# The scan of the state space layer: VectorE scales the last token tile of u times B, ScalarE the other seven

## The chip, the core and the metric

One core of a Trainium2 chip runs the whole program. The metric is the time of one execution on the device in microseconds (us). One execution was profiled; all rows of this document before the prediction come from it.

## The reference, cut to what matters

Four layers are chained, each with a residual: attention, a ternary feed-forward layer, a state space layer (Mamba) and a 2:4 sparse feed-forward layer. The change is in the third. Its input is (2, 1024, 256), there are 512 channels d and 16 states n:

```python
delta = softplus(dt_low @ dt_proj.T + bias)          # (b, l, 512)
deltaA = exp(delta[..., d] * A[d, n])                # decay per state
dBu = delta[b, l, d] * Bm[b, l, n] * x_conv[b, l, d] # drive per state
h = deltaA * h + dBu                                 # over the tokens l
y = sum over n of h * C[b, l, n]                     # then skip, gate, projection
```

With u = delta * x_conv, the drive of state n is u times B[:, n], one factor per token.

## The kernel before, in words

The two batches are worked off one after the other. Channels lie on the 128 partitions, in four tiles of 128; 1024 tokens lie along a row. A batch is scanned in two halves of two channel tiles each (e = 0, 1). A half has 16 states, in four rings (`it`) of four (`v`). One state of a half is a *pair* of two *units* (e = 0 and e = 1), so a batch has 32 pairs and 64 units, numbered by `unit`. For each unit:

- ScalarE, `decays` (L1424): the exponentials of 128x1024 into one of four buffers `m_da`. Semaphore `da_done`.
- ScalarE, `spread` (L1418): the factor B is one per token, so u is kept transposed (`m_uT`, tokens on the partitions, eight token tiles of 128x256 for both channel tiles) and each tile is scaled by one scalar per partition into `m_uB`, eight operations per pair. `m_uB` has two buffers; `spread` waits for `db_done`, the expands that read the buffer last. Semaphore `ub_done`, one count per tile.
- TensorE, `expand` (L907 to L914): eight transposes (128x128) bring the scaled tiles back to channels on partitions, into PSUM banks 4 to 7 (`drive(e)`). It waits for the scan that last read these banks, and with e = 0 before each transpose for its tile of `m_uB`. Semaphore `db_done`.
- VectorE, `state` (L2146 to L2156): a scan along the 1024 tokens, state = decay times state plus drive, into one of four buffers `m_h`. It waits for `da_done`, `db_done` and an add four units back. Semaphore `scan_done`.
- GpSimd (L2406): the product of the state with the row of C in place (`m_C`, one load by SyncE's queue per pair, L422). Semaphore `hc_done`.
- TensorE, `add_state` (L919): four matmuls with the identity add the product to y in PSUM. Semaphore `y_added`.

All engines work in the order in which their loops are written. On TensorE it is expand of a unit, then add of the unit two back. On VectorE it is scan after scan, and in half 1 the operations that finish the channels of half 0 stand between them: skip 0 and skip 1 (L2186, behind the first and the second scan of the half), gate 0 (L2192, before iteration 1), gate 1 (in iteration 1), low part 0 (L2196, before iteration 2), low part 1 (in iteration 2), and in batch 1 the statistics of the next layer before iteration 3. Gates and low parts read two tensors in SBUF, the skips one in SBUF and one in PSUM. ScalarE runs decays of pair v, then the spread of pair v + 1.

Elsewhere, VectorE and GpSimd meet in the attention layer: VectorE computes a bias row (L1531, a tensor times one scalar per partition) while GpSimd clips scores (L2279).

Of the kernel before, what the change touches and what calls it, by code (L numbers as in the profile page):

```python
# [12 lines left out]
ALU = mybir.AluOpType  # L13
# [4 lines left out]
B, S, D = 2, 1024, 256  # L18
KD = D // P
TILES = S // P  # L20
# [6 lines left out]
DI, DN, DR, DC = 512, 16, 128, 4  # L27
DT = DI // P
RING = 4
QUAD = 4  # L30
UNITS = 2 * B * TILES // QUAD
HALF_UNITS = DN * 2
# [8 lines left out]
def program(nc, x_in, slopes_in, wqk_in, wv_in, wo_in, wgu0_in, wp0_in, win_in, wx_in, wdt_in,  # L41
# [3 lines left out]
    with ctx:  # L45
# [82 lines left out]
        def causal_row(k):  # L128
# [72 lines left out]
        m_uT = place(t_mem, "m_uT", [P, 2, TILES, 2 * P])  # L201
# [63 lines left out]

        (mw_in, mw_hi, mw_lo, m_pad, m_in_full, m_in_read, m_z_read, m_tap, m_conv, m_silu, m_xc_hi, m_xc_lo, m_xd_full,
         m_xd_read, m_xd_lo, m_bc_out, m_dt_full, m_dt_act, m_sp, m_pre, bt_full, bt_read, ut_full, ut0_read, ut1_read,
         c_in0, c_in1, c_in2, c_in3, da_done, ub_done,
         db_done, scan_done, hc_done, y_added, y_skip, yz_done, y_hi, y_lo, m_o_full, m_o_added) = (
            sem(n) for n in (  # L270
                "mw_in", "mw_hi", "mw_lo", "m_pad", "m_in_full", "m_in_read", "m_z_read", "m_tap", "m_conv", "m_silu",
                "m_xc_hi", "m_xc_lo", "m_xd_full", "m_xd_read", "m_xd_lo", "m_bc_out", "m_dt_full", "m_dt_act",
                "m_softplus", "m_pre", "bt_full", "bt_read", "ut_full", "ut0_read", "ut1_read",
                "c_in0", "c_in1", "c_in2", "c_in3", "da_done", "ub_done", "db_done",
                "scan_done", "hc_done", "y_added", "y_skip", "yz_done", "y_hi", "y_lo", "m_o_full", "m_o_added"))
        c_in = (c_in0, c_in1, c_in2, c_in3)

# [16 lines left out]
        def unit(b, half, it, v, e):  # L294

            return it * (2 * RING) + ((2 * b + half) * HALF_UNITS + 2 * v + e)

        def drive(e):
            return ps[:, 4 + 2 * e:6 + 2 * e, :].rearrange("p a n -> p (a n)")
# [603 lines left out]
        def pe_mamba_scan(pe, b):  # L903

            def expand(half, it, v, e):

                n = unit(b, half, it, v, e)  # L907
                pe.wait_ge(scan_done, n + 3)
                for t in range(TILES):
                    if e == 0:  # L910
                        pe.wait_ge(ub_done, n * (TILES // 2) + (t + 1))
                    mm = nc.tensor.transpose(ps[:, 4 + 2 * e + t // 4, (t % 4) * P:(t % 4 + 1) * P],  # L912
                                             m_uB[:, v % 2, t, e * P:(e + 1) * P], ident[:, :])
                mm.then_inc(db_done, 1)  # L914

            def add_state(half, it, v, e, begin=False, end=False):
                pe.wait_ge(hc_done, unit(b, half, it, v, e) + 1)
                for c in range(2):
                    mm = nc.tensor.matmul(ps[:, 2 * e + c, :], ident[:, :],  # L919
                                          m_h[:, 2 * (v % 2) + e, c * BANK:(c + 1) * BANK],  # L920
                                          start=begin, stop=end)
                mm.then_inc(y_added, 1)

            last = DN // RING - 1
            for half in range(2):
                for e in range(2):
                    expand(half, 0, 0, e)
                    if half:
                        add_state(0, last, RING - 1, e, end=True)
                for v in range(1, RING):  # L930
                    for e in range(2):
                        expand(half, 0, v, e)
                        if half and v == 1:
                            pe.wait_ge(y_skip, DT * b + e + 1)
                        add_state(half, 0, v - 1, e, begin=(v == 1))
                with pe.Fori(1, last + 1) as it:
                    for v in range(RING):
                        for e in range(2):
                            expand(half, it, v, e)
                            if v:  # L940
                                add_state(half, it, v - 1, e)
                            else:
                                add_state(half, it - 1, RING - 1, e)
            for e in range(2):
                add_state(1, last, RING - 1, e, end=True)
                if b == B - 1:
                    pe.wait_ge(scan_done, 4 + 2 * B * HALF_UNITS)
                    pe_mamba_out(pe, b, (0, 1), range(4 * e, 4 * e + 4))
# [463 lines left out]
        def act_mamba_scan(act, b):  # L1412
            last = DN // RING - 1

            def spread(half, it, v):
                act.wait_ge(db_done, unit(b, half, it, v, 0) + 2)
                for t in range(TILES):
                    nc.scalar.activation(m_uB[:, v % 2, t, :], m_uT[:, half, t, :], ACT.Copy,  # L1418
                                         scale=m_bT[:, t, bass.ds(it * RING + v, 1)]).then_inc(ub_done, 1)

# [726 lines left out]
        def dve_mamba_scan(dve, b):  # L2147

            def state(half, it, v, es=range(2)):
                for e in es:  # L2150
                    n = unit(b, half, it, v, e)
                    dve.wait_ge(da_done, n + 1)
                    dve.wait_ge(y_added, n + 5)
                    dve.wait_ge(db_done, n + 5)
                    nc.vector.tensor_tensor_scan(m_h[:, 2 * (v % 2) + e, :], m_da[:, 2 * (v % 2) + e, :], drive(e),  # L2155
                                                 0.0, ALU.mult, ALU.add).then_inc(scan_done, 1)  # L2156

            with dve.Fori(0, DN // RING) as it:
                for v in range(RING):
                    state(0, it, v)  # L2160
            for e in range(2):
                state(1, 0, 0, (e,))
                dve.wait_ge(y_added, 8 + (2 * b + 1) * HALF_UNITS - 1 + e)
                dve_mamba_skip(dve, b, e)
            for v in range(1, RING):
                state(1, 0, v)
            dve_mamba_gate(dve, b, 0)
            for v in range(RING):
                state(1, 1, v)
                if v == 1:  # L2170
                    dve_mamba_gate(dve, b, 1)
                if v == 3:
                    dve_mamba_y_lo(dve, b, 0)
            for v in range(RING):
                state(1, 2, v)
                if v == 1:
                    dve_mamba_y_lo(dve, b, 1)
                if v == 3 and b == B - 1:
                    dve_sparse_stats(dve, 0)
            with dve.Fori(3, DN // RING) as it:  # L2180
                for v in range(RING):
                    state(1, it, v)

        def dve_mamba_skip(dve, b, e):
            at = 2 * (e % 2)
            nc.vector.scalar_tensor_tensor(m_xc[:, e, :], m_xc[:, e, :], skip_d[:, e:e + 1],  # L2186
                                           ps[:, at:at + 2, :].rearrange("p a n -> p (a n)"),
                                           ALU.mult, ALU.add).then_inc(y_skip, 1)
# [5 lines left out]
        def dve_mamba_y_lo(dve, b, e):  # L2194
            dve.wait_ge(y_hi, DT * b + e + 1)
            nc.vector.tensor_tensor(m_yl[:, e, :], m_xc[:, e, :], m_yh[:, e, :].bitcast(F32),  # L2196
                                    ALU.subtract).then_inc(y_lo, 1)
# [294 lines left out]
```

## Time and profile before

| | before |
|---|---|
| median of 3 runs | 1737.82 us (1734.57 to 1737.91) |
| the profiled execution | 1736.06 us, its span 1734.2 us |
| TensorE matmul / weight load | 1651.6 us (95%) / 1368.0 us (79%) |
| VectorE, ScalarE, GpSimd | 1395.4 (80%), 1266.7 (73%), 761.7 us (44%) |
| scan operation, VectorE | 128 times, mean 2.283 us, 291.0 us |
| product with C, GpSimd | 128 times, mean 2.422 us, 309.3 us |
| scaling of a token tile, ScalarE | 512 times, 210.6 us |
| chain that ended last | PE 62%, POOL 18%, DVE 10%, issue 6% of the span |

PE is TensorE, PEld its weight loads, DVE VectorE, ACT ScalarE, POOL GpSimd, SP SyncE. A row of the timeline has the start in us, the duration in us, the engine, the line, the operation with output and inputs, the count, and in brackets the idle time just before it with what released it. Where several instructions follow closely, one row holds them all.

### The profile page before, as it was taken

Reading aid. Unit: us, or ns where it says so; the run is one execution under the profiler, and the core shown is the slowest. Engines: PE = TensorE matmul, PEld = TensorE weight load, DVE = VectorE, ACT = ScalarE, POOL = GpSimd, SP = SyncE. Lnnn points to the kernel's source line nnn. Section 1 sums busy time; section 2 is a strip of 40 time slices with the busy share of each in tenths; the row PEclk is TensorE's granted clock in tenths of the full one; section 3 lists DMA queues with packets and bytes.
Section 4 is the critical chain, followed back from the end, with each engine's and each line's share of the span. In section 5 each row is a group of like instructions: output and inputs, shape, how many; then the busy total and the mean of one; then the engine's idle time right before and its main releaser. Section 6 shows DMA issues by size and latency. Waiting matters only on the chain.

```text
span 1734.2 us, 31419 instructions
## 1 busy us (share of the span) xinstructions
PE 1651.6 (95%) x9564; PEld 1368.0 (79%) x9564; DVE 1395.4 (80%) x2319; ACT 1266.7 (73%) x2380; POOL 761.7 (44%) x717
## 2 busy tenths in 40 slices
PE   8999999999999999999997997879999899999998
PEld 7899889998899889988995886656557656557887
DVE  7788877887787778777886665888988788888996
ACT  5777777777777777777774553899996799994442
POOL 4444435453544444444442111049893079881000
PEclk9999999999999999999999998989999999999999
DMA  2000000000000000000001000022220032240000
GB/s 99 31 20 19 30 24 18 18 30 24 16 16 28 24 21 11 25 24 27 9 0 50 1 0 0 4 85 98 97 97 13 13 112 97 98 138 8 13 13 25
DMA packets 25105, 64.13 MB, mean 37 GB/s; under 512 B 2832, under 2 KB 8976, under 8 KB 24784
## 3 DMA queue, kind: packets, MB, share of 16 engines
q1 hardware_dynamic: 25040, 63.31, 10.8%
q8 instruction: 36, 0.59, 0.1%
q14 instruction: 29, 0.24, 0.0%
HBM read 60.94 MB, written 2.36 MB: 36 GB/s over the span
## 4 chain that ended last, share of the span: by engine, by line
PE 62%; POOL 18%; DVE 10%; issue 6%; ACT 2%; DMA 1%; POOLq 0%; DVEq 0%; SPq 0%; ACTq 0%
POOL m_h L2406 15%; PE ps L565 11%; PE ps L527 10%; PE ps L550 7%; PE ps L482 7%; PE ps L578 5%; PE ps L505 5%; PE ps L781 4%; PE ps L697 3%; PE ps L793 2%; PE ps L718 2%; POOL prob L2286 1%; PE ps L957 1%; DVE m_delta L2096 1%; POOL prob L2279 1%
## 5 line engine op out<-in xcount | busy, mean ns | idle before, releaser
L2406 POOL TENSOR_TENSOR m_h<-m_h,m_C 128x1024 f32<-128x1024 f32 x128 | 309.3, 2422 | 174.2 <-DVE m_h L2155 173.6
L2155 DVE TENSOR_TENSOR_SCAN m_h<-m_y,ps 128x1024 f32<-128x1024 f32 x128 | 291.0, 2283 | 44.8 <-PE ps L912 42.8
L2286 POOL TENSOR_SCALAR prob<-prob,rinv 128x128 f32<-128x128 f32 (+7 forms) x256 | 228.4, 899 | 212.9 <-DVE rinv L1611 206.5
L2279 POOL TENSOR_SCALAR prob<-prob 128x128 f32<-128x128 f32 (+7 forms) x256 | 188.2, 735 | 286.2 <-ACT prob L1048 277.7
L919 PE MATMUL ps<-m_h,ident 128*128 128x512 f32 x512 | 246.0, 603 | 11.2 <-POOL m_h L2406 11.1
L1577 DVE TENSOR_TENSOR pt_lo<-ps,pt_hi 128x512 fp32r<-128x512 f32 (+2 forms) x320 | 189.6, 605 | 80.9 <-ACT pt_hi L1061 79.1
L1570 DVE CUSTOM_DVE_ANT_0 prob<-prob,bias 128x128 f32<-128x128 f32 (+7 forms) x256 | 214.0, 854 | 7.8 <-POOL prob L2279 4.6
L1048 ACT ACTIVATE prob<-ps 128x128 f32<-128x128 f32 (+7 forms) x256 | 165.7, 652 | 67.3 <-PE ps L527 66.7
L1061 ACT ACTIVATE pt_hi<-ps 128x512 fp32r<-128x512 f32 (+2 forms) x320 | 163.0, 531 | 66.4 <-PE ps L550 64.4
L1418 ACT ACTIVATE m_u<-m_uT,m_bT 128x256 f32<-128x256 f32 x512 | 210.6, 495 | 0.3 <-PE ps L912 0.2
L1054 ACT ACTIVATE prob<-prob,nmax 128x128 f32<-128x128 f32 (+7 forms) x256 | 198.1, 776 | 3.0 <-DVE nmax L1570 2.0
L912 PEld LDWEIGHTS ps<-ident,m_u 128*128 128x128 f32 x1024 | 122.7, 143 | 74.1 <-issue 60.6
L550 PE MATMUL ps<-ident,prob 128*128 128x128 f32 x1152 | 159.4, 274 | 7.1 <-POOL prob L2286 4.0
L550 PEld LDWEIGHTS ps<-ident,prob 128*128 128x128 f32 x1152 | 135.1, 141 | 29.2 <-issue 7.2
L919 PEld LDWEIGHTS ps<-m_h,ident 128*128 128x128 f32 x512 | 88.1, 192 | 79.7 <-issue 63.8
L527 PE MATMUL ps<-qk_hi 128*128 128x512 f32 (+2 forms) x384 | 143.4, 373 | 4.5 <-DVE v_lo L1583 2.4
L912 PE MATMUL ps<-ident,m_u 128*128 128x128 f32 x1024 | 136.5, 277 | 7.2 <-DVE m_uT L2143 5.0
L1424 ACT ACTIVATE m_y<-m_delta,negA 128x1024 f32<-128x1024 f32 x128 | 139.3, 1136 | 0.0
L527 PE MATMUL ps<-qk_hi,qk_lo 128*128 128x512 f32 (+2 forms) x384 | 131.9, 343 | 0.0
L527 PE MATMUL ps<-qk_lo,qk_hi 128*128 128x512 f32 (+2 forms) x384 | 131.4, 342 | 0.0
L565 PE MATMUL ps<-pt_hi,v_hi 128*128 128x512 f32 (+2 forms) x320 | 116.5, 364 | 0.0
L565 PE MATMUL ps<-pt_lo,v_hi 128*128 128x512 f32 (+2 forms) x320 | 115.7, 362 | 0.0
(257 smaller groups left out, 3961.7 us busy)
## 6 DMA issues: line engine op xcount, KB each, us to landing
m_C<-bc_dram SPq DMA_DIRECT2D x64, 512.0 KB, 3.6
wqk_raw<-wqk_in SPq DMA_DIRECT2D x16, 512.0 KB, 3.2
wv_raw<-wv_in SPq DMA_DIRECT2D x16, 256.0 KB, 2.6
wo_raw<-wo_in SPq DMA_DIRECT2D x16, 256.0 KB, 2.8
q_raw<-wgu_in SPq DMA_DIRECT2D x8, 256.0 KB, 2.7
raw<-wgu_in SPq DMA_DIRECT2D x1, 2048.0 KB, 8.0
out<-x SPq DMA_DIRECT2D x8, 256.0 KB, 2.1
x<-x_in SPq DMA_DIRECT2D x2, 512.0 KB, 4.3
```

Source lines behind the costliest of these rows:

```text
L527: mm = nc.tensor.matmul(flat[:, o + lo_c:o + hi_c], (qk_hi, qk_lo)[a][:, 2 * u, qt * P:(qt + 1) * P], (qk_hi, qk_lo)[w][:, 2 * u + 1, lo_c ...
L550: mm = nc.tensor.transpose(ps[:, 4 + idx % 2, r * P:(r + 1) * P], prob[:, at:at + P], ident[:, :])
L565: mm = nc.tensor.matmul(ps[:, 6 + g, c0:BANK], (v_hi, v_lo)[w][:, j, u * DH:(u + 1) * DH], cols, start=(j == 0 and i == 0), stop=(j == 4 * ...
L912: mm = nc.tensor.transpose(ps[:, 4 + 2 * e + t // 4, (t % 4) * P:(t % 4 + 1) * P], m_uB[:, v % 2, t, e * P:(e + 1) * P], ident[:, :])
L919: mm = nc.tensor.matmul(ps[:, 2 * e + c, :], ident[:, :], m_h[:, 2 * (v % 2) + e, c * BANK:(c + 1) * BANK], start=begin, stop=end)
L1054: nc.scalar.activation(prob[:, at:at + n], prob[:, at:at + n], ACT.Exp, bias=nmax[:, k:k + 1], scale=-1.0, accum_out=rsum[:, k:k + 1]).the ...
L1418: nc.scalar.activation(m_uB[:, v % 2, t, :], m_uT[:, half, t, :], ACT.Copy, scale=m_bT[:, t, bass.ds(it * RING + v, 1)]).then_inc(ub_done, 1)
L1570: nc.vector.tensor_tensor_reduce(out=tile, in0=tile, in1=bias[:, k // 8, S - n:S], scale=-1.0, scalar=BIG, op0=ALU.add, op1=ALU.min, accum ...
L2155: nc.vector.tensor_tensor_scan(m_h[:, 2 * (v % 2) + e, :], m_da[:, 2 * (v % 2) + e, :], drive(e), 0.0, ALU.mult, ALU.add).then_inc(scan_do ...
L2279: nc.gpsimd.tensor_scalar(prob[:, at:at + n], prob[:, at:at + n], CLIP, -CLIP, ALU.min, ALU.max).then_inc(s_clipped, 1)
L2286: nc.gpsimd.tensor_scalar(prob[:, at:at + n], prob[:, at:at + n], rinv[:, k:k + 1], 1.0, ALU.mult, ALU.mult).then_inc(norm_done, 1)
L2406: nc.gpsimd.tensor_tensor(state, state, m_C[:, v, :], ALU.mult).then_inc(hc_done, 1)
```

## The change

VectorE scales the eighth token tile, with a semaphore of its own, `ub_last`; ScalarE's loop ends at the seventh. On VectorE the scaling of pair v + 1 stands between the two scans of pair v (`both`) for v = 0 to 2. For v = 3 the scaling of the first pair of the next ring stands behind both scans. The loops over the rings are cut so that the last ring of a half is written out or ends without a scaling behind it. TensorE waits for `ub_done` before seven transposes and for `ub_last` before the eighth.

```diff
--- before.py
+++ after.py
@@ -265,13 +265,13 @@
 
         (mw_in, mw_hi, mw_lo, m_pad, m_in_full, m_in_read, m_z_read, m_tap, m_conv, m_silu, m_xc_hi, m_xc_lo, m_xd_full,
          m_xd_read, m_xd_lo, m_bc_out, m_dt_full, m_dt_act, m_sp, m_pre, bt_full, bt_read, ut_full, ut0_read, ut1_read,
-         c_in0, c_in1, c_in2, c_in3, da_done, ub_done,
+         c_in0, c_in1, c_in2, c_in3, da_done, ub_done, ub_last,
          db_done, scan_done, hc_done, y_added, y_skip, yz_done, y_hi, y_lo, m_o_full, m_o_added) = (
             sem(n) for n in (
                 "mw_in", "mw_hi", "mw_lo", "m_pad", "m_in_full", "m_in_read", "m_z_read", "m_tap", "m_conv", "m_silu",
                 "m_xc_hi", "m_xc_lo", "m_xd_full", "m_xd_read", "m_xd_lo", "m_bc_out", "m_dt_full", "m_dt_act",
                 "m_softplus", "m_pre", "bt_full", "bt_read", "ut_full", "ut0_read", "ut1_read",
-                "c_in0", "c_in1", "c_in2", "c_in3", "da_done", "ub_done", "db_done",
+                "c_in0", "c_in1", "c_in2", "c_in3", "da_done", "ub_done", "ub_last", "db_done",
                 "scan_done", "hc_done", "y_added", "y_skip", "yz_done", "y_hi", "y_lo", "m_o_full", "m_o_added"))
         c_in = (c_in0, c_in1, c_in2, c_in3)
 
@@ -294,6 +294,10 @@
         def unit(b, half, it, v, e):
 
             return it * (2 * RING) + ((2 * b + half) * HALF_UNITS + 2 * v + e)
+
+        def pair(b, half, it, v):
+
+            return it * RING + ((2 * b + half) * (HALF_UNITS // 2) + v)
 
         def drive(e):
             return ps[:, 4 + 2 * e:6 + 2 * e, :].rearrange("p a n -> p (a n)")
@@ -907,8 +911,10 @@
                 n = unit(b, half, it, v, e)
                 pe.wait_ge(scan_done, n + 3)
                 for t in range(TILES):
-                    if e == 0:
-                        pe.wait_ge(ub_done, n * (TILES // 2) + (t + 1))
+                    if e == 0 and t < TILES - 1:
+                        pe.wait_ge(ub_done, pair(b, half, it, v) * (TILES - 1) + (t + 1))
+                    elif e == 0:
+                        pe.wait_ge(ub_last, pair(b, half, it, v) + 1)
                     mm = nc.tensor.transpose(ps[:, 4 + 2 * e + t // 4, (t % 4) * P:(t % 4 + 1) * P],
                                              m_uB[:, v % 2, t, e * P:(e + 1) * P], ident[:, :])
                 mm.then_inc(db_done, 1)
@@ -1414,7 +1420,7 @@
 
             def spread(half, it, v):
                 act.wait_ge(db_done, unit(b, half, it, v, 0) + 2)
-                for t in range(TILES):
+                for t in range(TILES - 1):
                     nc.scalar.activation(m_uB[:, v % 2, t, :], m_uT[:, half, t, :], ACT.Copy,
                                          scale=m_bT[:, t, bass.ds(it * RING + v, 1)]).then_inc(ub_done, 1)
 
@@ -2155,31 +2161,61 @@
                     nc.vector.tensor_tensor_scan(m_h[:, 2 * (v % 2) + e, :], m_da[:, 2 * (v % 2) + e, :], drive(e),
                                                  0.0, ALU.mult, ALU.add).then_inc(scan_done, 1)
 
-            with dve.Fori(0, DN // RING) as it:
+            def spread_last(half, it, v):
+
+                dve.wait_ge(db_done, unit(b, half, it, v, 0) + 2)
+                dve.sem_inc(seen, 1)
+                nc.vector.tensor_scalar(m_uB[:, v % 2, TILES - 1, :], m_uT[:, half, TILES - 1, :],
+                                        m_bT[:, TILES - 1, bass.ds(it * RING + v, 1)], None,
+                                        ALU.mult).then_inc(ub_last, 1)
+
+            def both(half, it, v):
+
+                state(half, it, v, (0,))
+                if v < RING - 1:
+                    spread_last(half, it, v + 1)
+                state(half, it, v, (1,))
+
+            last = DN // RING - 1
+            dve.wait_ge(ut0_read, 2 * (b + 1))
+            dve.wait_ge(bt_read, b + 1)
+            spread_last(0, 0, 0)
+            with dve.Fori(0, last) as it:
                 for v in range(RING):
-                    state(0, it, v)
+                    both(0, it, v)
+                spread_last(0, it + 1, 0)
+            for v in range(RING):
+                both(0, last, v)
+            dve.wait_ge(ut1_read, 2 * (b + 1))
+            spread_last(1, 0, 0)
             for e in range(2):
                 state(1, 0, 0, (e,))
                 dve.wait_ge(y_added, 8 + (2 * b + 1) * HALF_UNITS - 1 + e)
                 dve_mamba_skip(dve, b, e)
+                if e == 0:
+                    spread_last(1, 0, 1)
             for v in range(1, RING):
-                state(1, 0, v)
+                both(1, 0, v)
+            spread_last(1, 1, 0)
             dve_mamba_gate(dve, b, 0)
             for v in range(RING):
-                state(1, 1, v)
+                both(1, 1, v)
                 if v == 1:
                     dve_mamba_gate(dve, b, 1)
                 if v == 3:
+                    spread_last(1, 2, 0)
                     dve_mamba_y_lo(dve, b, 0)
             for v in range(RING):
-                state(1, 2, v)
+                both(1, 2, v)
                 if v == 1:
                     dve_mamba_y_lo(dve, b, 1)
-                if v == 3 and b == B - 1:
-                    dve_sparse_stats(dve, 0)
-            with dve.Fori(3, DN // RING) as it:
+                if v == 3:
+                    spread_last(1, 3, 0)
+                    if b == B - 1:
+                        dve_sparse_stats(dve, 0)
+            with dve.Fori(last, DN // RING) as it:
                 for v in range(RING):
-                    state(1, it, v)
+                    both(1, it, v)
 
         def dve_mamba_skip(dve, b, e):
             at = 2 * (e % 2)
```

## Rows read from the trace of the kernel before

**Rows 1.** Windows: busy time (and count) of each engine in a steady stretch.

```profile
core 0: us, PE busy (x) PEld busy (x) DVE busy (x) ACT busy (x) POOL busy (x), PEclk, DMA share, GB/s
1156.00:1228.00 72.00, 72.00 (x333) 43.91 (x332) 63.44 (x29) 72.00 (x139) 65.57 (x28) 1.00 0.29 102
```

**Rows 2.** Timeline of all engines, steady stretch of half 0, batch 0.

```profile
1158.71 2.17 ACT L1424 ACTIVATE m_y<-m_delta,negA 128x1024 f32<-128x1024 f32 x2
...
1158.93 1.88 PE L919 MATMUL ps<-m_h,ident 128*128 128x512 f32 x4
1158.97 2.37 POOL L2406 TENSOR_TENSOR m_h<-m_h,m_C 128x1024 f32<-128x1024 f32 x1 [0.23 <-DVE m_h L2155]
1159.20 2.29 DVE L2155 TENSOR_TENSOR_SCAN m_h<-m_y,ps 128x1024 f32<-128x1024 f32 x1 [0.31 <-PE ps L912]
...
1160.65 1.04 PE L912 MATMUL ps<-ident,m_u 128*128 128x128 f32 x8
...
1160.79 3.29 ACT L1418 ACTIVATE m_u<-m_uT,m_bT 128x256 f32<-128x256 f32 x8
...
1161.52 1.88 PE L919 MATMUL ps<-m_h,ident 128*128 128x512 f32 x4
...
1161.79 2.29 DVE L2155 TENSOR_TENSOR_SCAN m_h<-m_y,ps 128x1024 f32<-128x1024 f32 x1 [0.31 <-PE ps L912]
...
1163.98 2.18 ACT L1424 ACTIVATE m_y<-m_delta,negA 128x1024 f32<-128x1024 f32 x2
```

**Rows 3.** Timeline around gate 0, batch 0.

```profile
1248.93 2.29 DVE L2155 TENSOR_TENSOR_SCAN m_h<-m_y,ps 128x1024 f32<-128x1024 f32 x1 [0.31 <-PE ps L912]
...
1251.13 1.20 DVE L2192 TENSOR_TENSOR m_xc<-m_xc,m_z 128x1024 f32<-128x1024 f32 x1
...
1251.29 7.99 POOL L2406 TENSOR_TENSOR m_h<-m_h,m_C 128x1024 f32<-128x1024 f32 x3 [0.23 <-DVE m_h L2155]
...
1252.25 4.46 DVE L2155 TENSOR_TENSOR_SCAN m_h<-m_y,ps 128x1024 f32<-128x1024 f32 x2
...
1254.61 1.98 PE L919 MATMUL ps<-m_h,ident 128*128 128x512 f32 x4 [0.63 <-POOL m_h L2406]
...
1257.30 1.88 PE L919 MATMUL ps<-m_h,ident 128*128 128x512 f32 x4
...
1260.19 2.29 DVE L2155 TENSOR_TENSOR_SCAN m_h<-m_y,ps 128x1024 f32<-128x1024 f32 x1 [0.30 <-PE ps L912]
```

**Rows 4.** Single lines: min/median/max ns; last row: a group (busy us, mean ns).

```profile
L1531 DVE TENSOR_SCALAR bias<-ramp,slopes x30: 737/744/1620, 58.4 to 892.7; 128x1024 f32<-128x1024 f32 x30
...
L1515 DVE TENSOR_SCALAR a_xn<-x,mv,rstd x8: 401/406/817, 28.6 to 31.3; 128x256 f32<-128x256 f32 x8
...
L2139 DVE TENSOR_TENSOR m_delta<-m_delta,m_l 128x1024 f32<-128x1024 f32 x8 | 9.8, 1225 | 0.3
```

**Rows 5.** Timeline in the attention layer, VectorE's bias row and GpSimd's clip.

```profile
892.70 1.62 DVE L1531 TENSOR_SCALAR bias<-ramp,slopes 128x1024 f32<-128x1024 f32 x1
892.73 1.04 POOL L2279 TENSOR_SCALAR prob<-prob 128x1024 f32<-128x1024 f32 x1
```

**Rows 6.** Timeline around skip 0, batch 0.

```profile
1231.43 1.26 DVE L2186 SCALAR_TENSOR_TENSOR m_xc<-m_xc,vecs,ps 128x1024 f32<-128x1024 f32 x1
...
1231.59 2.37 POOL L2406 TENSOR_TENSOR m_h<-m_h,m_C 128x1024 f32<-128x1024 f32 x1 [0.25 <-DVE m_h L2155]
...
1232.60 2.28 DVE L2155 TENSOR_TENSOR_SCAN m_h<-m_y,ps 128x1024 f32<-128x1024 f32 x1
...
1237.48 1.96 PE L919 MATMUL ps<-m_h,ident 128*128 128x512 f32 x4 [0.54 <-POOL m_h L2406]
```

**Rows 7.** Windows at the start of the scan of batch 0, columns as in rows 1.

```profile
1145.80:1149.20 3.40, 1.84 (x11) 1.01 (x9) 3.39 (x2) 3.40 (x8) 2.11 (x1) 1.00 0.18 75
1149.20:1152.60 3.40, 3.09 (x4) 1.41 (x5) 2.29 (x1) 3.40 (x8) 3.32 (x3) 0.51 0.00 0
```

**Rows 8.** What VectorE's scans (L2155) waited for: us, times.

```profile
  ACT m_y L1424: 2.0, 6
```

## The prediction

> **What bounds the kernel now.** I read the shares of the page first: TensorE is the busiest engine. The change touches only the scan of the two batches (slices 27 to 36 of 40), so everything else is read there. The windows say who has no air in it: in a stretch of 72.00 us TensorE and ScalarE are both busy 72.00 us, VectorE 63.44, GpSimd 65.57 [rows 1]. The timeline of a steady stretch says which of the two sets the pace [rows 2]. A unit is half a state pair: the expand (eight transposes) starts at 1160.65, the add (four matmuls) at 1161.52, and one add follows the other by 2.59 us (1158.93, 1161.52), as do the scans (1159.20, 1161.79). ScalarE repeats every 5.27 us for two units (1158.71 to 1163.98), 2.635 per unit. A different period, so the units are not paced by ScalarE: it runs ahead and loses 0.09 us a pair of its lead. That TensorE's 2.59 is its own rate and not a latency shows after a gate: adds at 1254.61, 1257.30 and no wait before the second [rows 3]. VectorE idles 0.30 us before each scan; GpSimd's product ends at 1158.97 + 2.37 = 1161.34, 0.18 before its add. So a unit has 0.30 us of air on VectorE, about 0.1 on GpSimd and none on TensorE.
>
> **What is removed.** The two batches have 64 pairs (128 units), and each pair loses one of ScalarE's eight scalings: 3.29/8 = 0.41 us [rows 2], 26 us in all. Nobody waits for them: ScalarE is ahead, and its period drops to 4.87, under TensorE's 5.19. Worth 0.
>
> **What is added, in the common place.** For states 0 to 2 of a ring of four, VectorE's scaling (128x256, one scalar per partition) stands between the two scans of the pair in front. Its price: the bias operation has the same form with 1024 elements and takes 0.744, while a tensor by tensor operation of that size takes 1.225, so it moves two elements in the time of one [rows 4]. Its 1024 elements take 0.55 (what it still had to do when it had been held up, see the gates below), so 768 fewer cost 0.41 less: 0.33, rounded up to 0.34. Above stands the normalisation of the same tile with two scalars, 0.406; below, the part of the bias row that doesn't grow with its length, 0.744 - 0.55 = 0.19. I take 0.34, from the row of the same form. An operation that is ready starts 2.20 us after the scan's start (1248.93 to 1251.13) and the next 0.08 before its end (1251.13 + 1.20 to 1252.25) [rows 3]. So the scaling runs from 2.20 to 2.54, and the second scan could start at 2.46, before its turn at 2.59. Hidden by VectorE's idle time. Its wait (the expands that read the buffer two pairs back) was met two units earlier; nothing is queued behind it but the second scan. The counting and address instructions that come with it are not in these rows; they can run while the first scan streams for 2.29 us, so 0, and up to 0.13 would still be covered. TensorE counts two semaphores where it counted one: 0, hidden by its own matmuls. No DMA is moved; the rows of C wait for adds and shift with them.
>
> On GpSimd the product of the first scan would start at 2.36, inside the scaling. How that is paid is seen at the gate: the product issued at 1251.29 while the gate ran (to 1252.33), and the add behind it started at 1254.61, 2.28 after the gate's end [rows 3]. Here that gives 2.54 + 2.28 = 4.82; the add's turn is at 2.37 + (1161.52 - 1158.97) = 4.92. Hidden, with 0.1 to spare. The Trainium skill (SBUF — State Buffer, section Who interferes with whom) has a harder rule: a VectorE operation on both ports locks GpSimd out for the whole instruction. By it the add would start at 2.54 + 2.37 + 0.05 = 4.96, 0.04 late, at most 0.04 x 32 = 1.3 us more; the gate's row shows an overlap of about 0.15 instead.
>
> **At the end of a ring.** For the first state of the next ring the scaling is written behind the *second* scan, and its reader is the expand that runs during that very scan. That expand starts 1160.65 - 1159.20 = 1.45 into the scan, its eighth transpose at 1.45 + 0.77 = 2.22 (1.04 less one transpose of 0.27 leaves seven steps of 0.11). The tile is done at 2.54, plus a signal of 0.07 (scan end 1251.22 to GpSimd 1251.29), plus a restart of 0 to 0.10 (adds that waited take 1.98, others 1.88 [rows 2, 3]): 0.39 to 0.49 late, I take 0.43. TensorE is in order: the add behind is late too, and with no air nothing gives it back. With the price between 0.19 and 0.406 the stall is 0.24 to 0.56. Places per batch: three rings of half 0, the change of halves, and the rings of half 1 before iterations 1, 2, 3: seven. Two of these have a VectorE operation behind them that reads two tensors (gate 0, low part 0); these are the next part. The very first scaling of a batch runs while TensorE is at its first seven transposes: 0, and 0.34 at most. Five remain: 5 x 0.43 = 2.15 per batch (in batch 1 the statistics stand behind the last, with one input; VectorE's 0.26 more there, the same order).
>
> **Gate 0 and low part 0.** Today the gate starts before GpSimd's product (1251.13, 1251.29) and wins the port. Behind the scaling it can be issued only at 2.46, and the product has stood there since 2.36. Who comes second waits: a bias operation was issued at 892.70, a clip of GpSimd's at 892.73; VectorE's took 1.62 instead of 0.744 and ended 0.55 after GpSimd's end (893.77) [rows 4, 5]. Being issued 0.03 ahead didn't help it, so 0.10 behind will not. Counted from the start of the scan in front: product over at 2.54 + 2.28 less 0.05 for the signal, so about 4.76; gate does its 1024 elements at one each, 0.55 x 2 = 1.08, and ends at 5.84; the next scan starts at 5.76 (now 3.32) and ends at 8.05; the scaling behind it ends at 8.31, its product lets the add go at 8.31 + 2.28 = 10.59, where it now starts at 1257.30 - 1248.93 = 8.37. With the restart the scan two further on is 2.3 late (now 1260.19). The stall of 0.43 lies inside. Two per batch: 4.6.
>
> **Between the skips.** The scaling for state 1 stands behind skip 0, ready at 1232.60, in the middle of the product that runs from 1231.59 to 1233.96 [rows 6]. It waits for that end and needs 0.55/4 = 0.14 more: 1234.10, so the second scan starts at 1234.02 and not 1232.60: 1.42. VectorE is the chain here (the add at 1237.48 waited 0.54 for the product of that scan), so it is passed on: 1.45 with the restart.
>
> **Sum.** 2.15 + 4.6 + 1.45 = 8.2 per batch, 16.4 for both. The profiled execution took 1736.06 (span 1734.2 and 1.9 around it): 1752.5. The three runs have a median of 1737.82, 1.76 more, which gives 1754.2. I forecast **1754**. What follows the scans is released by their last results and moves along.
>
> **Rivals.**
> (a) The clock. After a stretch with TensorE busy 1.84 of 3.40 us at granted 1.00, the next was granted 0.51 (1.2 GHz), and held four matmuls, work of 1.88 us at 2.4 GHz [rows 2, 7]. At the gate and low part TensorE would now stand idle some 2.6 of 3.5 us. Each fall costs up to 1.7: with one to four, 1756 to 1761. Against: idle spells of 0.63 left it at full speed. 0.2.
> (b) The port is no obstacle to gate and skip (the gate keeps it from the scaling, or the scaling takes none). Then a batch loses 5 x 0.43 at ring ends, 0.26 between the skips (the scaling's own time) and at the two gates some 0.15 each, since the late tile falls into TensorE's present wait of 0.63: 2.7, and 5.4 in all. That is 1741.5 from the profiled execution and 1743 from the median. For: gates of before were never locked out for long. Against: rows 5. 0.15.
> (c) GpSimd wins the port in every pair: the scaling then waits for a product of 2.37, some 1.9 us lost in 64 pairs, 120 us, 1858. Its point: the product issued less than some 0.1 after the scaling; it is 0.16. 0.04.
> (d) Not slower: ScalarE is the true bound and TensorE's expand its follower, so that a late eighth tile costs nothing and 0.41 a pair comes off its work. It decides if the eighth scaling ends later than the transposes reach it. For: its 72.00 busy of 72.00 [rows 1]. Against: the two periods differ, and all scans together waited 2.0 us for its decays [rows 8]. That is also about the most to be had: 1735 to 1738. 0.06.
> The rest, 0.05, are mixtures beyond the range. My forecast: 0.5.
>
> **Range.** 1742 (rival b with the cheap scaling) to 1762 (rival a in full); c, d and some mixtures are out, about 0.15. A measurement of this kernel tells about 0.2%, 3.5 us, from no change. Faster 0.02, same 0.05 (d), slower 0.93.
>
> **What would show it.** Steady scans still 2.59 apart inside a ring, and about 3.02 at every ring's end, with TensorE waiting for VectorE's scaling; ScalarE with idle time; scalings of 0.34; gate 0 and low part 0 some 3.4 us long by the row (issued, then waiting) and the scan behind 2.4 later; the scaling between the skips 1.5 long; TensorE's granted clock at 1.00 through both events. Wrong it would be if scans at ring ends stay 2.59 apart, or if gates still take 1.20.

## The result and the profile after

The changed kernel takes **1757.08 us** (median of 4 runs, 1755.75 to 1758.18), the kernel before beside it 1736.81 (4 runs, 1734.57 to 1737.91): a ratio of 1.0123, 95% interval 1.011 to 1.0135, 20 us slower. The forecast was 1754, with 1742 to 1762 as its range. The profiled execution took 1756.45, its span is 1754.7 us.

The head of the page after, with its first part:

```profile
span 1754.7 us, 31475 instructions
## 1 busy us (share of the span) xinstructions
PE 1660.4 (95%) x9564; PEld 1369.7 (78%) x9564; DVE 1422.6 (81%) x2383; ACT 1249.2 (71%) x2316; POOL 761.2 (43%) x717
```

VectorE has 64 instructions more (2319 before), ScalarE 64 fewer: the change does what it says. These shares tell nothing of the 20 us. The steady stretch of [rows 1], as windows of the kernel after, does:

```profile
1156.00:1228.00 72.00, 71.37 (x331) 43.51 (x330) 65.33 (x41) 67.98 (x122) 64.33 (x28) 1.00 0.29 102
```

TensorE, busy 72.00 of 72.00 before, now misses 0.63; ScalarE misses 4.02. The timeline (start, duration, what it waited for) shows where TensorE's 0.63 lies: first two places inside a ring, then the ring's end.

```profile
1156.72 2.29 DVE L2161 TENSOR_TENSOR_SCAN m_h<-m_y,ps 128x1024 f32<-128x1024 f32 x1 [0.31 <-PE ps L918]
...
1158.92 0.33 DVE L2168 TENSOR_SCALAR m_u<-m_uT,m_bT 128x256 f32<-128x256 f32 x1
...
1159.09 2.39 POOL L2442 TENSOR_TENSOR m_h<-m_h,m_C 128x1024 f32<-128x1024 f32 x1 [0.22 <-DVE m_h L2161]
...
1159.31 2.29 DVE L2161 TENSOR_TENSOR_SCAN m_h<-m_y,ps 128x1024 f32<-128x1024 f32 x1
...
1164.50 2.29 DVE L2161 TENSOR_TENSOR_SCAN m_h<-m_y,ps 128x1024 f32<-128x1024 f32 x1 [0.30 <-PE ps L918]
...
1165.95 0.93 PE L918 MATMUL ps<-ident,m_u 128*128 128x128 f32 x7
1166.70 0.33 DVE L2168 TENSOR_SCALAR m_u<-m_uT,m_bT 128x256 f32<-128x256 f32 x1
...
1167.08 0.33 PE L918 MATMUL ps<-ident,m_u 128*128 128x128 f32 x1 [0.21 <-DVE m_u L2168]
...
1167.52 2.29 DVE L2161 TENSOR_TENSOR_SCAN m_h<-m_y,ps 128x1024 f32<-128x1024 f32 x1 [0.49 <-PE ps L918]
```

Inside a ring, scaling and second scan fit: 1156.72 to 1159.31 is the old 2.59. At the ring's end the scaling is issued at 1166.70, when seven of the eight transposes have been issued; the eighth waits for it, and the next scan comes 1167.52 - 1164.50 = 3.02 after the last. Gate 0 and low part 0 (the group for [rows 3]):

```profile
1254.57 0.45 DVE L2168 TENSOR_SCALAR m_u<-m_uT,m_bT 128x256 f32<-128x256 f32 x1
1254.94 3.39 DVE L2228 TENSOR_TENSOR m_xc<-m_xc,m_z 128x1024 f32<-128x1024 f32 x1
...
1277.31 2.29 DVE L2161 TENSOR_TENSOR_SCAN m_h<-m_y,ps 128x1024 f32<-128x1024 f32 x1 [0.31 <-PE ps L918]
1279.51 0.33 DVE L2168 TENSOR_SCALAR m_u<-m_uT,m_bT 128x256 f32<-128x256 f32 x1
1279.67 2.40 POOL L2442 TENSOR_TENSOR m_h<-m_h,m_C 128x1024 f32<-128x1024 f32 x1 [0.23 <-DVE m_h L2161]
1279.75 3.40 DVE L2232 TENSOR_TENSOR m_yl<-m_xc,m_yh 128x1024 fp32r<-128x1024 f32 x1
1283.07 2.27 DVE L2161 TENSOR_TENSOR_SCAN m_h<-m_y,ps 128x1024 f32<-128x1024 f32 x1
```

The gate takes 3.39 instead of 1.20, the low part 3.40. "Locked out" below means just this: issued second at the port of the prediction, and waiting inside one's own row. The low part ends at 1283.15, that is 1.08 after GpSimd's product (1279.67 + 2.40 = 1282.07): it did its 1024 elements when the product was over. The next scan starts 5.76 after the one in front (1277.31 to 1283.07). And between the skips (for [rows 6]):

```profile
1233.41 1.26 DVE L2222 SCALAR_TENSOR_TENSOR m_xc<-m_xc,vecs,ps 128x1024 f32<-128x1024 f32 x1
1233.58 2.37 POOL L2442 TENSOR_TENSOR m_h<-m_h,m_C 128x1024 f32<-128x1024 f32 x1 [0.66 <-DVE m_h L2161]
1234.59 1.51 DVE L2168 TENSOR_SCALAR m_u<-m_uT,m_bT 128x256 f32<-128x256 f32 x1
1236.02 2.27 DVE L2161 TENSOR_TENSOR_SCAN m_h<-m_y,ps 128x1024 f32<-128x1024 f32 x1
```

The scaling takes 1.51 and ends 0.15 after the product (1235.95). The view of its line says how often TensorE's matmuls waited for it, of 64 times:

```profile
L2168 DVE TENSOR_SCALAR m_u<-m_uT,m_bT x64: 321/328/1514, 1142.5 to 1575.2; 128x256 f32<-128x256 f32 x64
...
who waited for it (us, times):
...
  PE ps L918: 3.3, 14
```

Fourteen times: the seven ring ends of two batches. The last part lies in TensorE's clock, which fell in places where it had not fallen before. Windows behind gate 0 of batch 1 (the fields are those of [rows 1]; the third from the end is the granted clock), and below it at that batch's start:

```profile
1514.70:1518.10 3.40, 1.51 (x9) 1.25 (x10) 3.40 (x4) 3.36 (x6) 2.75 (x2) 1.00 0.48 154
1518.10:1521.50 3.40, 3.40 (x7) 1.47 (x6) 2.14 (x2) 0.73 (x1) 3.40 (x2) 0.51 0.00 0
```

```profile
1402.10:1405.50 3.40, 2.95 (x5) 1.36 (x6) 3.26 (x3) 3.40 (x6) 3.33 (x2) 0.50 0.04 13
1405.50:1408.90 3.40, 3.40 (x11) 2.27 (x10) 0.40 (x2) 3.40 (x7) 2.38 (x1) 0.50 0.00 0
```

In the wake of the gate TensorE was busy 1.51 of 3.40 us, and then worked 3.40 us at 1.2 GHz. At the batch's start the clock was at 1.2 GHz for 6.8 us; the kernel before had one stretch of 3.4 after its first scan there (1395.0), and another around the start of that scan (1388.2 to 1391.6, the scan at 1390.63), which the kernel after does not have.

A third place lies behind the scans, at the first matmuls of the next layer. TensorE stands idle there in both kernels alike; in the kernel after, the clock then falls. After, and below it before:

```profile
1600.10:1603.50 3.40, 1.04 (x7) 0.78 (x7) 3.40 (x4) 0.00 (x0) 0.00 (x0) 1.00 0.00 0
1603.50:1606.90 3.40, 3.40 (x10) 2.62 (x9) 1.70 (x3) 0.00 (x0) 0.00 (x0) 0.50 0.02 5
```

```profile
1581.37:1584.77 3.40, 1.04 (x7) 0.78 (x6) 3.40 (x4) 0.00 (x0) 0.00 (x0) 1.00 0.00 0
1584.77:1588.17 3.40, 3.40 (x17) 2.79 (x16) 2.04 (x4) 0.60 (x1) 0.00 (x0) 1.00 0.02 5
```

**Measuring the steps.** Every scan start is a row of the trace, so each place can be read by itself: the time between two scans of one number, after less before. Gate 0 of batch 0, scans 40 and 48: 1252.37 to 1277.31 is 24.94, before 1248.93 to 1271.45 is 22.52: 2.4 more. The same for all places (us more than in the kernel before, batch 0 / batch 1; "start" is scans 1 to 8, "ring ends" scans 8 to 33, "skips" 33 to 40, "gates" 40 to 48, "low parts" 48 to 56, "last ring" 56 to 64):

| kernel | start | ring ends | skips | gates | low parts | last ring | sum |
|---|---|---|---|---|---|---|---|
| after | 0.18 / 1.39 | 1.87 / 1.88 | 1.45 / 1.44 | 2.41 / 3.80 | 2.29 / 2.28 | 0.51 / 0.29 | 8.73 / 11.09 |
| e10, after again | 0.06 / 1.37 | 1.88 / 1.89 | 1.45 / 1.45 | 2.39 / 3.79 | 2.29 / 2.29 | 0.50 / 0.29 | 8.58 / 11.07 |
| e1 | -0.03 / 1.37 | 0.06 / 0.06 | 1.45 / 1.45 | 0.02 / -0.16 | 0.00 / 0.01 | 0.03 / 0.04 | 1.54 / 2.77 |
| e2 | -0.03 / 0.03 | 1.87 / 1.89 | 1.67 / 1.45 | -0.02 / -0.18 | 0.01 / 0.01 | 0.51 / 0.30 | 4.00 / 3.50 |
| e5 | 0.17 / -0.04 | 0.06 / 0.06 | 0.29 / 0.29 | 0.00 / -0.16 | 0.00 / 0.00 | 0.04 / 0.04 | 0.57 / 0.19 |
| e9 | -0.03 / 0.12 | 1.87 / 1.87 | 0.51 / 0.28 | 0.01 / -0.17 | 0.00 / 0.00 | 0.50 / 0.29 | 2.86 / 2.38 |
| e3b | -0.04 / 1.35 | 0.08 / 0.07 | 1.47 / 2.45 | 2.30 / 2.10 | 3.89 / 3.97 | 0.06 / 0.29 | 7.76 / 10.22 |
| e4 | 1.41 / 0.14 | 0.00 / 0.00 | 0.00 / 0.00 | 0.02 / -0.01 | 0.01 / -0.01 | 0.00 / 0.01 | 1.44 / 0.13 |
| e6 | 0.02 / 0.07 | 0.00 / 0.00 | 0.01 / 0.00 | 7.14 / 6.95 | 6.22 / 6.20 | 0.00 / 0.00 | 13.38 / 13.23 |
| e7 | -0.07 / 1.26 | 0.00 / 0.00 | 0.00 / 0.00 | -1.58 / -1.77 | -1.58 / -1.59 | 0.75 / 0.56 | -2.47 / -1.55 |
| e8 | 0.04 / 1.48 | 0.07 / 0.06 | 0.29 / 0.29 | -1.55 / -1.38 | -1.58 / -1.58 | 0.40 / 0.57 | -2.34 / -0.56 |

The first row holds 19.8 of the 20.4 us by which the span grew. The rest lies outside the scans. From the last scan of batch 0 to the first of batch 1 it is 0.96 less, where the kernel before has the extra low stretch, so of the 1.39 at batch 1's start only 0.4 is left. Behind the last scan it is 1.64 more, and that is the third fall of the clock. The same part reads 1.62 in e10, 1.58 in e3b and 1.46 in e9, each with a fall at the same matmuls, and 0.04 or less in the others, which have none. The -0.16 or so of several kernels at the gates of batch 1 is the kernel before's: its gate 1 there took 1.38 us, its other three gates in the scans 1.20.

### The profile page after: what moved, and what is told of

Its sections match the earlier page's. It is cut to its first block, busy times and chain, and to the rows that moved or that the text cites. A ratio compares the mean times of both kernels' runs of the same rounds, so it can differ in the third digit from the quotient of the medians.

```text
span 1754.7 us, 31475 instructions
## 1 busy us (share of the span) xinstructions
PE 1660.4 (95%) x9564; PEld 1369.7 (78%) x9564; DVE 1422.6 (81%) x2383; ACT 1249.2 (71%) x2316; POOL 761.2 (43%) x717
## 4 chain that ended last, share of the span: by engine, by line
PE 62%; POOL 18%; DVE 10%; issue 7%; ACT 2%; DMA 1%; POOLq 0%; DVEq 0%; SPq 0%; ACTq 0%
POOL m_h L2442 15%; PE ps L569 11%; PE ps L531 10%; PE ps L554 7%; PE ps L486 7%; PE ps L582 5%; PE ps L509 5%; PE ps L785 4%; PE ps L701 3%; PE ps L797 2%; PE ps L722 2%; POOL prob L2322 1%; PE ps L963 1%; DVE m_delta L2102 1%; POOL prob L2315 1%
## 5 line engine op out<-in xcount | busy, mean ns | idle before, releaser
L1424 ACT ACTIVATE m_u<-m_uT,m_bT 128x256 f32<-128x256 f32 x448 | 185.8, 495 | 31.8 <-PE ps L918 31.2
L918 PE MATMUL ps<-ident,m_u 128*128 128x128 f32 x1024 | 140.2, 278 | 15.1 <-DVE m_uT L2149 5.0
```

## Experiments

**e1, e2, e4: take the parts away.** e1 moves every ring-end scaling in between the two scans of the ring's last pair; the engines' work is that of the change:

```diff
                 state(half, it, v, (0,))
                 if v < RING - 1:
                     spread_last(half, it, v + 1)
+                elif ahead is not None:
+                    spread_last(*ahead, 0)
                 state(half, it, v, (1,))
...
-            spread_last(1, 1, 0)
             dve_mamba_gate(dve, b, 0)
```

> The changed kernel, but the scaling for the next ring stands between the two scans of the last state, as it does for the other states; the one between the skips stays. Theory (late tile at ring ends plus lockout at gate 0 and low part 0): all 14 ring-end losses go, 10 x 0.43 and 4 x 2.3 us, and the 2 x 1.45 between the skips stay: 1736.8 + 2.9, about 1740 us. Scans across ring ends 2.59 apart, gate 0 back at 1.20. Rival (the port is lost in all pairs, wherever the scaling stands): stays near 1755.

Measured: 1738.24 us (10 runs), ratio 1.0013 (1.0003 to 1.0023). The gate is back at 1.20, in a kernel that has the same scalings (timeline of e1):

```profile
1251.65 0.33 DVE L2168 TENSOR_SCALAR m_u<-m_uT,m_bT 128x256 f32<-128x256 f32 x1
1252.04 2.29 DVE L2161 TENSOR_TENSOR_SCAN m_h<-m_y,ps 128x1024 f32<-128x1024 f32 x1
1254.24 1.20 DVE L2224 TENSOR_TENSOR m_xc<-m_xc,m_z 128x1024 f32<-128x1024 f32 x1
```

e2 makes this move only for the two scalings ahead of gate 0 and low part 0 in each batch.

> Only the scalings in front of gate 0 and low part 0 are moved between the scans (4 of the 14 ring ends); the other 10 stay. Theory: 4 x 2.3 us go, and the fall of the clock behind gate 0 of batch 1 with them: about 1745 to 1748 us. Rival (all ring ends cost the same, the gates nothing of their own): 1757 - 4 x 1.2, about 1752.

Measured: 1742.88 (6 runs), ratio 1.0042 (1.0029 to 1.0055). The ring ends stay at 1.87, the gates and low parts fall to 0. The change less e2, by their ratios: 1.0123 - 1.0042 = 0.0081, 14 us. Of these, 11.0 lie at the gates and low parts of the table (some 1.5 of them the clock's). Most of the rest is the other clock stretches, at the start of batch 1 and behind the scans, which e2's profile does not have; that the four scalings bring them is not shown. That is in part why e2 came out below the 1745 expected; the kernel before, at 1735.54 beside it, was 1.3 lower as well.

e4 is the relief alone: ScalarE scales seven tiles, VectorE none, and the eighth tile is written once per batch by two activations of ScalarE (so the drive of the last 128 tokens repeats that of the first two states).

```diff
-                for t in range(TILES):
+                for t in range(TILES - 1):
...
+            for r in range(2):
+                nc.scalar.activation(m_uB[:, r, TILES - 1, :], m_uT[:, 0, TILES - 1, :], ACT.Copy,
+                                     scale=m_bT[:, TILES - 1, r:r + 1]).then_inc(ub_last, 1)
             spread(0, 0, 0)
```

> ScalarE's side of the change alone: the kernel before, with seven scalings per pair; the eighth tile of both buffers is written once per batch and then reused, so the drive of the last 128 tokens is wrong for all but the first states. VectorE gets no scaling. Theory (ScalarE never sets the pace): 1736.8 us, no change beyond 1 us. Rival d (ScalarE is the bound): up to 3 us faster or more.

Measured: 1737.2 (10 runs), ratio 1.001 (1.0001 to 1.002). All its places read -0.01 to 0.02 but the starts, 1.41 and 0.14; batch 0 has a longer stretch at 1.2 GHz there. Taking 26 us of work from ScalarE buys nothing: rival (d) has fallen.

**e3b: VectorE's time and port without a late tile.** ScalarE scales all eight tiles, TensorE waits for those alone; VectorE's scalings stay in the change's places and write into scratch.

```diff
-                for t in range(TILES - 1):
+                for t in range(TILES):
...
-                nc.vector.tensor_scalar(m_uB[:, v % 2, TILES - 1, :], m_uT[:, half, TILES - 1, :],
+                nc.vector.tensor_scalar(m_dump[:, :], m_uT[:, half, TILES - 1, :],
```

> The other half of e4: ScalarE makes all eight scalings again, and VectorE does the change's scalings too, at the change's places, into a scratch tile that nobody reads (63 of 64; the first of each batch is left out). TensorE waits for ScalarE's tiles alone. So nobody can be late for the tile; what is left is VectorE's own time and the port it shares with GpSimd. Theory (the port): ring ends cost 0, gate 0 and low part 0 still run about 3.4 us and cost 2.3 each, between the skips 1.45: 6.05 per batch, 12.1 in all, and 1736.8 + 12.1 = 1748.9, in the range 1747 to 1751. Rival (the late tile alone makes the loss at the gates too): only 1.45 between the skips or nothing, 1737 to 1740.

Measured: 1753.57 (4 runs), ratio 1.0104 (1.0089 to 1.012). Above the range, but not by the stalls: ring ends 0.08 and 0.07, gate 0 2.30 and 2.10, skips 1.47 in batch 0. Gate 0 in its timeline:

```profile
1251.94 0.33 DVE L2168 TENSOR_SCALAR m_dump<-m_uT,m_bT 128x256 f32<-128x256 f32 x1
...
1252.10 2.40 POOL L2443 TENSOR_TENSOR m_h<-m_h,m_C 128x1024 f32<-128x1024 f32 x1 [0.22 <-DVE m_h L2160]
1252.18 3.40 DVE L2229 TENSOR_TENSOR m_xc<-m_xc,m_z 128x1024 f32<-128x1024 f32 x1
```

So the gate's 2.3 is the port's alone: nobody waits for the tile here. What the expectation lacked is the clock: behind low part 0 it fell in both batches, and the places there read 3.89 and 3.97 instead of 2.29. It fell also behind the skips of batch 1 (at 1493.2; the skips read 2.45) and behind the scans (1.58). Windows of e3b, low part 0 of batch 0:

```profile
1281.60:1285.00 3.40, 1.13 (x8) 0.95 (x8) 3.40 (x4) 2.71 (x6) 2.32 (x1) 1.00 0.44 154
1285.00:1288.40 3.40, 3.28 (x4) 1.39 (x5) 2.62 (x3) 1.15 (x1) 3.34 (x3) 0.50 0.00 0
```

**e6: the suspected cost, doubled.** The kernel before, with one scaling into scratch, which nobody reads, ahead of each gate and low part; nothing else is changed.

```diff
+            aside()
             dve_mamba_gate(dve, b, 0)
...
+                    aside()
                     dve_mamba_y_lo(dve, b, 1)
```

> The kernel before, ScalarE with all eight scalings, and one VectorE scaling (128x256 into scratch that nobody reads) directly ahead of each of gate 0, gate 1, low part 0 and low part 1: eight in all, no other change. Theory (port lost to the product, once per place): gate 0 and low part 0 take 3.4 instead of 1.20 and the next scan starts 2.3 late; gate 1 and low part 1 stand behind the second scan of their ring's place as well and lose the same: 8 x 2.3 = 18.4, so 1755, range 1753 to 1759 with falls of the clock. If only those places are hit where the product is issued ahead of the gate: 4 x 2.3 = 9.2, 1746. Rival (a scaling costs its own 0.26 to 0.34 and no more): 1738 to 1740.

Measured: 1762.1 (4 runs), ratio 1.016 (1.0145 to 1.0176). All four of a batch are locked out; by form, for batch 0:

```profile
L2206 DVE TENSOR_TENSOR m_yl<-m_xc,m_yh 128x1024 fp32r<-128x1024 f32 x2 | 6.8, 3396 | 0.0
L2202 DVE TENSOR_TENSOR m_xc<-m_xc,m_z 128x1024 f32<-128x1024 f32 x2 | 6.8, 3393 | 0.0
```

That gives 4 x 2.3 = 9.2 per batch, as expected; measured are 13.4 and 13.2, and the time lies above the 1753 to 1759 of the expectation. The other 4.2 are again stretches at 1.2 GHz, 6.8 us behind gate 1 and 3.4 behind low part 0, in both batches alike, none of which the kernel before has in these places. So 3.4 us at the low clock cost some 4.2/3 = 1.4 us here, and 0.33 us of VectorE work in such a place costs 3.3 us with the clock counted in.

**e5 and e9: the rest in its parts.** e5 is e1 with the scaling for state 1 ahead of skip 0 instead of behind it.

```diff
                 state(1, 0, 0, (e,))
+                if e == 0:
+                    spread_last(1, 0, 1)
                 dve.wait_ge(y_added, 8 + (2 * b + 1) * HALF_UNITS - 1 + e)
                 dve_mamba_skip(dve, b, e)
-                if e == 0:
-                    spread_last(1, 0, 1)
```

> e1 and one move more: the scaling for state 1 of half 1 stands ahead of skip 0 instead of behind it, so that it is done when GpSimd's product begins. The work and the engines are those of the change; only 16 of its 64 scalings stand elsewhere. Theory: e1 was 1.44 per batch too long, at the skips alone (2.9 in all with 0.5 of the clock); skip 0 comes 0.34 later and loses at most its own 0.3, so 0 to 0.7 is left: 1736 to 1738, ratio 1.000 to 1.001. Rival (the scaling's own place doesn't matter there; skip 0 is locked out in its turn): 1738 to 1740 as e1.

Measured: 1736.34 (10 runs), ratio 1.0007 (0.9997 to 1.0016). The skips fall from 1.45 to 0.29, about one scaling's own time, and skip 0 is not locked out:

```profile
1231.68 0.33 DVE L2168 TENSOR_SCALAR m_u<-m_uT,m_bT 128x256 f32<-128x256 f32 x1
...
1231.85 2.40 POOL L2438 TENSOR_TENSOR m_h<-m_h,m_C 128x1024 f32<-128x1024 f32 x1 [0.22 <-DVE m_h L2161]
...
1231.93 1.27 DVE L2218 SCALAR_TENSOR_TENSOR m_xc<-m_xc,vecs,ps 128x1024 f32<-128x1024 f32 x1
```

The skip reads one of its inputs from ps, where the gate reads both from SBUF; otherwise it stands as the gate did, behind a scaling and 0.08 behind GpSimd's product. The Trainium skill (SBUF — State Buffer, section Who interferes with whom) names two SBUF inputs as what makes a VectorE instruction contend with GpSimd's reads; the 1.27 here beside the gates' 3.39 agrees.

e9 keeps only the five ring ends of the sum (and those alone) in the change's place.

> The change with the scalings ahead of gate 0, low part 0 and behind skip 0 moved in between the scans as in e5; the other five ring ends of each batch (and only these) keep the change's place behind the second scan. Theory: 5 x 0.43 per batch, 4.3 in all, on e5's 1736.3: 1740.6, range 1739.5 to 1742. Rival (the tile isn't late there, and e5's gain was the gates' and the skip's alone): 1736 to 1737.

Measured: 1742.42 (4 runs), ratio 1.0046 (1.0028 to 1.0063). The places read 1.87 and 0.50 or 0.29, 4.5 us for both batches. The time is somewhat above the expected range. Its ratio less e5's is 0.0039, 6.8 us; in its profile 1.46 of that is the fall of the clock behind the scans (at 1588.4), which e5's does not have. Its four runs lie from 1739.99 to 1744.82, so the places, not the medians, are what tells.

**e10: does the clock's part repeat?** The changed kernel, unchanged.

> The changed kernel once more, unchanged, for the clock's part. Theory: the placed stalls (five ring ends, gate 0, low part 0, between the skips) repeat to 0.1 us, 8.2 to 8.7 per batch without a clock fall; the rest of the distance to before is stretches of granted clock 0.5 at the start of a batch's scan or behind a gate, 1.4 us for each 3.4 us of them, and these may lie elsewhere this time: 1755 to 1758. Rival (the fall behind gate 0 of batch 1 belongs to the program): it is there again at the same distance from the batch's first scan, and not in batch 0.

Measured: 1753.89 (4 runs) beside 1733.53 of before, ratio 1.0115 (1.0099 to 1.0131). The fall behind gate 0 of batch 1 is there again, 119.8 us after the batch's first scan (1514.8 - 1395.04; in the first profile 1518.1 - 1398.33 = 119.8), and not in batch 0:

```profile
1511.40:1514.80 3.40, 1.52 (x9) 1.25 (x10) 3.40 (x4) 3.36 (x6) 2.76 (x2) 1.00 0.48 154
1514.80:1518.20 3.40, 3.40 (x7) 1.45 (x6) 2.12 (x2) 0.73 (x1) 3.40 (x2) 0.50 0.00 0
```

Here the rival of the expectation is right: in both profiles the fall belongs to the same place. So does the one behind the scans, 205.2 and 205.1 us after batch 1's first scan. The stretch at the start of batch 1 (1.37) came back too, but e1, e3b, e7 and e8 (and e4 in batch 0) have it as well and e2, e5, e9 and e6 don't, and e7 has no scaling of VectorE's at all: it is not the change's.

**e7 and e8: is the relief worth something in a faster kernel?** e7 is the kernel before with gates and low parts cut (quarters, thirds), a piece behind each pair of half 1 from the third on; two operations of ScalarE (the high parts) move with them. e8 adds the change's division in e5's places.

```diff
+            for p in range(1, DN):
+                it, v = p // RING, p % RING
+                state(1, it, v)
+                if p >= 2 and work:
+                    f, e, lo, hi = work.pop(0)
+                    f(dve, b, e, lo, hi)
```

> The kernel before, ScalarE with all eight scalings and no scaling on VectorE; the gates are cut into four quarters and the low parts into three pieces, and one piece stands behind each pair of half 1 from the third pair on, instead of a whole one at four places (the high parts of ScalarE are moved one ring earlier or later to match). Theory: a whole gate or low part costs the unit about 1.2 less 0.3 of VectorE's air, so 4 x 0.7 to 0.9 per batch; pieces of 0.3 to 0.4 fit the air nearly. Gain 5 to 7 of which ScalarE's lead of 0.09 a pair lets through some 5: 1730 to 1732. Rival (each piece loses the port to the product as the scaling did in front of the gate, 14 pieces of 0.3 to 2.3): 1740 or more.

> The pieces of e7 together with the change's division of the scalings, all 64 of VectorE's between two scans as in e5. In e7 the scans gained 3.2 us per batch by the pieces and then gave back 0.5 to 0.8, at a scan that waited 0.47 us for ScalarE's decays: its lead was used up. Theory (ScalarE is next behind TensorE, and 0.41 a pair is worth something only once the units run faster): what was given back stays, 1 to 1.6 us in the two batches, so 1729.5 to 1730.5, ratio to before about 0.997. Rival (VectorE's air is used twice, a scaling and a piece in one pair: 0.26 + 0.33 against 0.60): the pairs of half 1 stretch and it is 1731 to 1735.

Measured: e7 1731.17 (9 runs), ratio 0.9976 (0.9966 to 0.9986); e8 1731.32 (11 runs), ratio 0.9982 (0.9973 to 0.9991), in another set of runs. Both beat both kernels, the one before by 0.2%; the relief adds nothing. VectorE in e7 and, below it, in e8, at the same pairs:

```profile
1292.47 2.29 DVE L2154 TENSOR_TENSOR_SCAN m_h<-m_y,ps 128x1024 f32<-128x1024 f32 x1 [0.30 <-PE ps L912]
1294.67 0.48 DVE L2185 TENSOR_TENSOR m_yl<-m_xc,m_yh 128x336 fp32r<-128x336 f32 x1
1295.63 2.29 DVE L2154 TENSOR_TENSOR_SCAN m_h<-m_y,ps 128x1024 f32<-128x1024 f32 x1 [0.47 <-ACT m_y L1424]
```

```profile
1290.76 2.29 DVE L2160 TENSOR_TENSOR_SCAN m_h<-m_y,ps 128x1024 f32<-128x1024 f32 x1
1292.96 0.48 DVE L2217 TENSOR_TENSOR m_yl<-m_xc,m_yh 128x336 fp32r<-128x336 f32 x1
1293.53 2.29 DVE L2160 TENSOR_TENSOR_SCAN m_h<-m_y,ps 128x1024 f32<-128x1024 f32 x1
1295.73 0.33 DVE L2167 TENSOR_SCALAR m_u<-m_uT,m_bT 128x256 f32<-128x256 f32 x1
1296.12 2.29 DVE L2160 TENSOR_TENSOR_SCAN m_h<-m_y,ps 128x1024 f32<-128x1024 f32 x1
```

e7's wait of 0.47 for ScalarE is gone in e8, as the theory said, but no scan waits for TensorE either: a pair with scaling and piece takes 1296.12 - 1290.76 = 5.36, where TensorE's is 5.19. The air of VectorE is spent, as its rival said. What held back e7's last ring (0.75 and 0.56) beyond that one wait was not tried.

## Why the prediction was right

Direction, size and places were right, and the median lies 3.1 us above the forecast. The stalls that the sum adds up measured 16.8 us (forecast 16.4). The growth was 20.3 by the medians; the forecast stood on 1737.82 for the kernel before, 1.0 above the 1736.81 beside the result, and by that luck the miss looks smaller.

- **Worth 0: ScalarE's relief.** Shown by e4, place by place.
- **The common place, 0.** Right: 2.59 inside the rings, and 0.06 us a batch over the whole of half 0 in e1. The scaling cost 0.33 (forecast 0.34). The product issued during it (1159.09) took 2.39, 0.02 more than [rows 2]. The Trainium skill's rule (SBUF — State Buffer, section Who interferes with whom) that GpSimd is locked out for the whole instruction would have made it 0.16 longer, to 1159.25, and 2.53: the row speaks for the overlap that was read from the gate.
- **Ring ends, 0.43.** Right: 3.02 - 2.59, and TensorE's matmuls waited for the scaling at ring ends only. Four of them make 1.87 (forecast 1.72); the fifth is 0.50 in batch 0 and 0.29 in batch 1. e3b, without a late tile, has 0.08. So the mechanism is the late tile and no cost of VectorE's.
- **Gate 0 and low part 0, 2.3 each.** Right: 2.41 and 2.29; the scan behind starts 5.76 after the one in front, as worked out for it. e3b and e6 show it to be the port alone, e1 and e2 that it goes with the scaling's place.
- **Between the skips, 1.45.** Right to 0.01, and 0.29 when the scaling is issued before the product.
- **What the sum left out is the clock.** It had no term for it; the prediction put it into rival (a) as "one to four" falls of up to 1.7 at gates and low parts, and expected a granted clock of 1.00 through both. The profile shows one such fall, behind gate 0 of batch 1: the place reads 3.80 instead of 2.41, 1.4 us. So rival (a) came true in its smallest form beside the forecast's stalls, and 1757.08 lies in its 1756 to 1761. Another fall, behind the scans, was named by nobody and cost 1.64. Together with some 0.5 for the shifted stretches at the two batch starts, and the 0.4 by which the stalls were undersized (0.25 at the ring ends, 0.2 at the gates and low parts), these make the 4.0 by which the span's growth of 20.4 exceeds 16.4. Idle of TensorE at the gates had been named as what would bring a fall; the chance of 0.2 was too small, since e3b and e6 have falls of this kind in both batches.

## What to carry to other kernels

Work that an idle engine could take costs by where it is put, not by its length: here 64 scalings of 0.33 us cost 20 us in one order (16.8 of stalls, the rest with the clock) and nothing measurable in another, because a short one pushes the instruction behind it from 0.16 us ahead of GpSimd's 2.4 us operation to 0.08 behind it, on the same port, and another makes TensorE's eighth tile late. Before moving work, look up who starts in the quarter of a microsecond after each place, and who reads the result while it is made; then put it where neither is so. And relieving an engine that is full by its busy time is worth nothing as long as another paces it.

## What the runs showed of the hardware

- Order at the port turns on a quarter of a microsecond. A gate issued 0.16 ahead of the product takes 1.20 [rows 3]; issued 0.08 behind it (1252.18 and 1252.10 in e3b) it takes 3.40, and [rows 5] have one that was 0.03 ahead and lost. VectorE's row starts at issue, so a lockout shows as a longer instruction and not as idle time.
- An idle spell of TensorE can cost twice: as itself, and as 3.4 us at 1.2 GHz behind it, 1.0 to 1.7 us in these kernels (1.0 at e3b's skips, 1.4 by e6, 1.64 behind the scans, 1.6 to 1.7 at e3b's low parts). How long TensorE is idle does not tell whether it does. Behind the scans it was busy 1.04 of 3.40 us in both kernels, and only in the kernel after did the clock fall. Behind gate 0 the clock fell in batch 1 in both profiles of the changed kernel and in batch 0 in neither, although TensorE's idle is the same: this is batch 0's stretch at the same distance from its gate's issue, 5.08 us, as the one with 1.51 busy at 1514.70.

```profile
1260.02:1263.42 3.40, 1.50 (x9) 1.24 (x10) 3.40 (x4) 3.36 (x6) 2.77 (x2) 1.00 0.39 154
```

The clock stays at full speed for the rest of that batch. Why the two batches differ was not settled.
